# Three read-outs of a block moved behind the level products of the next unit, in TensorE's order

## The reference, cut to what matters

```
xn = layernorm(x);  sx = token_shift(xn, ctx[:, 1])
xxx = tanh((xn + sx * maa_x) @ maa_w1) @ maa_w2          # five low-rank mixes
x5 = xn + sx * (maa_stack + xxx)
w = exp(-exp(time_decay + tanh(x5[1] @ decay_w1) @ decay_w2))
r, k, v, g = x5[3] @ Wr.T, x5[0] @ Wk.T, x5[2] @ Wv.T, silu(x5[4] @ Wg.T)
for t:  a = k_t v_t';  out_t = r_t (u * a + s);  s = a + w_t * s      # per head, 128 steps
x = x + (groupnorm(out) * g) @ Wo.T
xn2 = layernorm(x); token shift; xk, xr
x = x + sigmoid(xr @ ffn_Wr.T) * (relu(xk @ ffn_Wk.T) ** 2 @ ffn_Wv.T)
```

## Time and profile before

| | us |
|---|---|
| median of three runs | 1507.39 (1506.85 to 1512.62) |
| the profiled execution | 1505.76 |
| its span | 1504.0 |
| TensorE matmuls busy | 1438.4 (96%) |
| VectorE busy | 909.6 (60%) |
| GpSimd busy | 599.2 (40%) |
| ScalarE busy | 517.6 (34%) |

### The profile page before, as it was taken

One profiled execution on the slowest core, in us unless ns is written; L12 is line 12 of the kernel. 1 busy time (PEld: TensorE's weight loads), 2 busy tenths in 40 slices (PEclk: granted clock), 3 DMA queues, 4 the chain that ended last, 5 costly groups with the idle time before them and its releaser, 6 DMA issues.

```text
span 1504.0 us, 51989 instructions
## 1 busy us (share of the span) xinstructions
PE 1438.4 (96%) x22954; PEld 1071.4 (71%) x22954; DVE 909.6 (60%) x1990; ACT 517.6 (34%) x911; POOL 599.2 (40%) x528
## 2 busy tenths in 40 slices
PE   8998999999999999999999999999999999999898
PEld 7776876767777676876767777676876767777464
DVE  3667557664675657657574775656657564665542
ACT  1323433323333333432433333333423433332332
POOL 3353516235362433616235362433616235262421
PEclk9999999999999999999999999999999999999899
DMA  8011101011110111101011010111102011010110
GB/s 311 7 49 44 41 26 57 17 41 54 32 59 7 41 54 38 55 22 61 18 41 54 29 56 13 41 55 38 55 10 73 17 41 54 14 55 15 57 31 28
DMA packets 56448, 68.11 MB, mean 45 GB/s; under 512 B 23264, under 2 KB 40032, under 8 KB 55200
## 3 DMA queue, kind: packets, MB, share of 16 engines
q1 hardware_dynamic: 56224, 64.79, 13.9%
HBM read 43.75 MB, written 8.39 MB: 35 GB/s over the span
## 4 chain that ended last, share of the span: by engine, by line
PE 81%; DVE 9%; SPq 4%; issue 2%; DMA 2%; ACT 1%; POOL 1%; DVEq 0%; ACTq 0%; POOLq 0%
PE pairs L1227 31%; PE pairs L1246 20%; PE at_ps L1155 4%; PE pairs L1238 4%; SPq L404 3%; PE at_ps L1148 3%; DVE x L781 3%; PE pairs L1254 3%; PE pairs L1270 2%; PE att_ps L1218 2%; PE pairs L1293 2%; PE pairs L1338 1%; PE pairs L1311 1%; PE pairs L1305 1%; DVE sx L881 1%
## 5 line engine op out<-in xcount | busy, mean ns | idle before, releaser
L1227 PE MATMUL pairs<-x,wts 128*128 128x256 f32 x1760 | 397.0, 380 | 1.1 <-DVE lag L805 0.4
L1227 PEld LDWEIGHTS pairs<-x,wts 128*128 128x128 f32 x1760 | 328.4, 190 | 51.2 <-issue 7.1
L978 ACT ACTIVATE at<-at_ps 128x512 f32<-128x512 f32 x128 | 76.4, 597 | 381.5 <-PE at_ps L1155 190.3
L551 POOL TENSOR_TENSOR x<-x,xnT 128x1024 f32<-128x1024 f32 (+1 forms) x79 | 158.5, 2006 | 63.4 <-DVE x L781 63.4
L781 DVE SCALAR_TENSOR_TENSOR x<-pairs,vecs,sx 128x256 f32<-128x256 f32 x316 | 129.0, 474 | 82.2 <-PE pairs L1270 72.1
L561 POOL TENSOR_TENSOR bonv<-bonv,lag 128x256 f32<-128x256 f32 x32 | 27.1, 847 | 226.8 <-DVE lag L801 226.8
L1227 PE MATMUL pairs<-yT,wts 128*128 128x256 f32 x512 | 113.8, 380 | 3.1 <-POOL yT L551 1.9
L1155 PE MATMUL at_ps<-rm,kc 128*16 128x128 f32 (+1 forms) x2048 | 111.8, 276 | 3.9 <-issue 3.9
L1246 PE MATMUL pairs<-wts,cen 128*128 128x512 f32 x240 | 107.2, 598 | 4.5 <-DVE x L781 4.5
L1246 PE MATMUL pairs<-wts,yT 128*128 128x512 f32 x240 | 107.1, 599 | 0.5 <-POOL yT L588 0.5
L1227 PEld LDWEIGHTS pairs<-yT,wts 128*128 128x128 f32 x512 | 95.9, 190 | 16.1 <-issue 2.0
(11 more groups left out here) (198 smaller groups left out, 2621.0 us busy)
## 6 DMA issues: line engine op xcount, KB each, us to landing
rm<-rst SPq DMA_DIRECT2D x1024, 12.0 KB, 1.8
xu<-in_x SPq DMA_DIRECT2D x16, 512.0 KB
wts<-in_wts SPq DMA_DIRECT2D x8, 1024.0 KB, 14.0
kvs<-in_s SPq DMA_DIRECT2D x32, 256.0 KB, 2.9
s<-in_s SPq DMA_DIRECT2D x32, 256.0 KB, 3.8
x<-in_x SPq DMA_DIRECT2D x15, 512.0 KB, 4.9
out<-sx SPq DMA_DIRECT2D x15, 512.0 KB, 3.0
prev<-in_prev SPq DMA_DIRECT2D x32, 4.0 KB, 3.6
```

The costliest lines, as they stand in the source:

```text
L551: gp.tensor_tensor(t, t, old, ALU.add).then_inc(x5_ready, 1)
L978: ac.activation(at[:, :, :], at_ps[:, :].rearrange("p (h t) -> p h t", h=HG), ACT.Copy)\
L1227: last = pe.matmul(ps[:, g // 2, TB * (g % 2):TB * (g % 2 + 1)], wts[:, m, k, g * P:(g + 1) * P], source[:, k, :], start=(k == 0), stop=(k ...
```

## The change

V0, V1 and V2 each move one place later among the units: V0 from before wv.0 to directly behind A1, V1 from before hs_1 to directly behind A2, V2 from directly behind A2 to directly behind A3. No other engine's order and no wait in the code changes.

```
-PE_ORDER = ["kt0", "V7", "hs_0", "kv0", "A0", "mixWV", "aT1", "V0", "wv.0", "wv.1", "A1", "vt_1", "V1", "hs_1", "A2", "V2",
- "v.0", "v.1", "A3", "mixKR", "kt1", "V3", "z", "kv1", "k.0", "yT", "k.1", "decay", "A4", "mixG", "aT0", "r.0",
+PE_ORDER = ["kt0", "V7", "hs_0", "kv0", "A0", "mixWV", "aT1", "wv.0", "wv.1", "A1", "V0", "vt_1", "hs_1", "A2", "V1",
+ "v.0", "v.1", "A3", "V2", "mixKR", "kt1", "V3", "z", "kv1", "k.0", "yT", "k.1", "decay", "A4", "mixG", "aT0", "r.0",
  "xT", "r.1", "A5", "V4", "wo.0", "wo.1", "g.0", "A6", "V5", "x2T", "g.1", "h", "A7", "V6", "vt_0", "kk.0",
  "kk.1", "rr.0", "rr.1"]
```

## The result

The changed kernel takes 1521.41 us against 1507.57 us before (medians of four runs): a ratio of 1.0087 with a 95% interval of 1.0062 to 1.0113, about 13 us slower. Measured a second time it gave 1.0087 (1.0069 to 1.0106). The prediction of 1515 us (1509 to 1520) had the sign and half of the size; the result lies above its high end.

The account below looks back on a forecast made before the run. TensorE carries 81% of the chain, but other engines only just let it proceed at some steps. 13 x 0.59 = 7.7, less 1.1, plus 1.0 = +7.6 us on the median 1507.39: 1515.0 us, range 1509 to 1520.

Parts of the forecast that it names:

- all four pins: In a block, wv.0, hs_1 and v.0 wait for banks other engines free; mixKR starts behind A3 alone, 0.59 us later.
- TensorE's own work: Rival: no bank wait holds, so each block saves 1.24 us, 19 us over fifteen, giving 1489; chance 0.05.
- the bank that doesn't bind: Rival: at v.0 only V2's wait bound, so a block costs +0.12 us, +2 to +3 in all, 1510; chance 0.09.
- GpSimd's bound: Rival: later ScalarE work delays GpSimd's tail up to k.0, 0.3 us a block, 4 us more, 1519; chance 0.13.
- the rule weighed in the prediction: Changing tiling mode drains TensorE, so a level and read-out standing together save 0.22 us a pair; alone, a gain.
- the agreement "in size": The trace's saving of 0.22 us a pair was said to agree in size with the skill's drain at mode changes.
- 1.1 us come back: At v.0, issue gaps that had delayed it are won back, 1.1 us over the thirteen full blocks.
- the clock at no cost: In the full blocks, the forecast sum had no clock term; a clock under 1.00 there would show it wrong.
- the clock rival: Rival: new waits lower the granted clock; 4 us at half clock cost 2 us a block, 1541 in all; chance 0.05.
- the first two blocks: These blocks have no wv; 0.5 us more was taken for each, between 0 and 1.2, 1.0 in the sum.
- The first offset: Before the change, the median 1507.39 was 1.6 us above the profiled execution of 1505.76; the forecast was put on its scale.

Follow-up runs that it names:

- the short chain: The changed kernel with two VectorE operations cut to one group each, leaving out part of the products: ratio 1.0060 (1.0043 to 1.0076).

## Why the prediction was wrong, point by point

- **Right:** all four pins. wv.0 at 2.97 (2.98 predicted to stay), hs_1 at 13.25 (13.16), v.0 at 16.16 (16.17), mixKR at 25.04 (25.05), line 532 not moved. The clear block is 0.59 us longer, 7.7 us in thirteen. V2 alone carries it, and the short chain shows that line 805 pins v.0. Of the rivals, TensorE's own work, the bank that doesn't bind and GpSimd's bound are out. The Trainium skill, "TensorEngine Tiling (Array Packing)", Performance Considerations, says that the emptying of PSUM may bound where tiling has made TensorE faster; the trace agrees at mixWV, whose matmuls use 32 rows each: they take 1.17 us, VectorE's eight reads of them 3.23 us, and wv.0 waits 1.02 us for the first four. The other two pins are of another kind: vt_1 uses all 128 rows and columns, and VectorE comes to hs_1 only 0.4 us after its end. Of the rule weighed in the prediction, the saving was there (A1 with V0 takes 1.77 us, 0.22 less than 1.18 and 0.81) but fell behind the pins. The page gives no size for a drain, so the agreement "in size" was not one, and no run here shows that the drain is the cause.
- **Wrong, the term "1.1 us come back":** I took the gaps in front of v.0 as something of before that the new idle time would swallow. Instead they cost 3.0 and 2.4 us in the two traces (1.2 before), and 0.7 to 0.8 more in v: some 2.5 us lost instead of 1.1 won. In the changed order A2 and V1 leave only 0.4 us of slack, less than a gap of 1.3. The gaps sit at fixed places in the stream, and a new order puts other steps under them. The three places in front of v.0 lie in A2 in before, with gaps of 0.1, 0 and 0.5 us, and in V1 in the change, with 1.3, 1.3 and 0.5. For the first two of them the packet of instructions begins 12.3 and 11.5 us behind mixWV in before, but 14.8 and 14.7 in the change; why it comes later stays open.
- **Wrong, the clock at no cost:** I let the clock rival be decided by the length of one wait, and the wait alone indeed never lowered it. Together with an issue gap just before, it did in some cases: 4.3 and 3.4 us in two blocks of each trace. Why one such pair lowers it and the next doesn't stays open, and so does what the dummies in that wait did. The rival was right in kind, in two blocks of thirteen instead of all. As an either-or case with 1541 us it left the range no room for the partial case.
- **Too small in these traces, the first two blocks:** 0.5 us each were assumed; the two traces show 3.5 to 4.0 in the first and nothing in the second. Over all traces some 1.5 of it seems to be the order, which is near the 1.0 assumed.
- **The sum:** 7.7 + 4.3 (clock) + 2.5 (gaps between A2 and the end of v, where -1.1 stood) + 3.5 (first block) - 1.1 (other gaps, fewer than before) = 16.9 us, of 18.0 that the trace of the change has over that of before. The medians differ by 13 to 14, since the profiled execution of before was 1.8 us faster than its median and that of the change 2.6 us slower. The first offset I had noted and added as if it were the same for both.

## What to carry to other kernels

Work that fills a wait is not cost, and to move it away saves nothing: ask of each step what pins the one behind it, and count a move only where the pin is TensorE itself. Then leave room for gaps that no semaphore explains. Here they stood at fixed places in the instruction stream, where TensorE waited for its next 256 instructions. They cost nothing where a wait covers them, and more than their length where they meet an idle time and the clock falls. To know such a gap, look whether it ends at a fixed time behind a packet of the instruction queue. To fill a wait with dummy matmuls may be worth a try; here the kernel with them was faster by 5 us at the ratios' middle, and it isn't shown that the filling did it.

## What the runs showed of the hardware

TensorE's instructions came in packets of 16 KB, 256 instructions each. Issue gaps of 0.3 to 1.7 us stood only at one place in these 256, about every fourth block at the same step, and ended 1.1 to 1.6 us after a packet's end (120 gaps in thirteen traces). They moved one block when 68 instructions were added ahead and not at all when 256 were. Idle times of 1.0 us alone left the clock at 1.00 in every clear block. An issue gap of 0.56 us and a wait of 1.21 us that ended 2.3 us apart had it at 0.50 right behind, but such a pair did so in 9 of 27 cases only: with 64 dummies at the start, wv.0 came 1.6 us late once and wv still ran at full speed.
